# Removing the unread products from TensorE's waits at the ends of two attentions and the starts of two expert stages

## The chip, the cores and the metric

The program runs on one core of one Trainium2 chip. The metric is the device time of one execution in microseconds (us); the kernel before is given by the median of three executions. TensorE runs at one of two clocks here, 1.2 or 2.4 GHz; the profile calls them a granted clock of 0.50 and 1.00.

## The reference

Two transformer layers over x (8 batches, 100 tokens, width 512) with a context of 722 rows per batch. Each layer is a cross attention and a routed feed-forward with a residual around each:

```python
x = x + _L0_xattn_ref(_layernorm(x), ctx_1024, ...)   # 16 heads of 32, causal mask: 100 keys count
x = x + _L0_ffn_ref(_layernorm(x), ...)               # router, best 2 of 8 experts, gelu, width 2048
x = x + _L1_xattn_ref(_layernorm(x), ctx_1024, ...)   # 16 heads of 64, 100 own keys and 722 of the context
x = x + _L1_ffn_ref(_layernorm(x), ...)               # router, best 2 of 8 experts, silu(gate)*up, width 1024
```

## The kernel before, in words

Five stages follow one another, each a block in which every engine has its own written-out program, with a barrier of all engines between blocks: `front` (attention 0 and the routing of its tokens), `experts` for layer 0, `project` (queries, keys and values of layer 1), `attend` (attention 1 and its routing) and `experts` for layer 1; `finish` normalises the last rows.

Precision is kept by splitting float32 operands into a rounded high part and the remainder (`hi`, `lo`) and adding three products. TensorE's program order is the order of the code; where it waits for a semaphore, everything behind stands still.

`front` walks over the batches b = 0 to 7. For one batch TensorE makes the scores (L549, L554), half of the projection of a later pair (`project_half`, L533, only for b up to 5), the values (`values`, 12 products of 512 columns at L511), the router's logits of batch b - 2 (`route_logits`, L617), the output projection of batch b - 1 (`output`, again L511), a rank (`route_rank`, L623 and L624), the transposes of the probabilities (L578), the attended values (L592, L597) and the transposes of the router's rows (`route_turn`, L608). For b = 6 and 7 there is no projection left, and the gap before `values`, which waits for VectorE's `a_y` (the scaled attended rows of the batch before, semaphore `yn`), is filled by `idle_products(6, wo[0])`. Behind the loop come the output of batch 7 and the routing of batches 6 and 7, with three more such calls. An unread product is a matmul into a bank of which nobody reads the result; the bank is written afresh by the next real product with `start=True`:

```python
def idle_products(n, wide):
    for _ in range(n):
        nc.tensor.matmul(ps[:, 7, :], wide[:, 0, 0:128], wide[:, 1, :], start=True, stop=True)
```

What follows the last rank is serial: VectorE turns it into slots, GpSimd scatters the rows to DRAM (`scatter`, L476), SyncE waits for these and loads the first 256 rows of the first expert pass (L434, `e_xs`), and TensorE's `turn(0)` of the next block waits for them.

`experts` runs passes of 256 rows. Ahead of the loop TensorE transposes the first rows (`turn(0)`, 8 transposes at L1157), VectorE and ScalarE copy and split them (L1262 or L1259, L1358, L1268, the last giving `e_xl`), and the first real product (L1188, 256 columns) waits for `e_xl`. In that gap stand 14 unread products of 512 columns (L1171). In a pass each block `kb` is 12 products of 256 columns per up matrix (L1188) and, three blocks later, 6 products of 512 columns (L1165).

`attend` runs over 64 head pairs. After the last one come the last attended values (L2151), the last three products of the output projection (L2168), then the routing of batch 7: `route_turn` (L2187), `route_logits` (L2197), `route_rank` (L2206, L2207). Between these stand 4, 3, 12 and 10 unread products of 362 columns (L2180).

Of the kernel before, what the change touches and what calls it, by code (L numbers as in the profile page):

```python
# [132 lines left out]
def after(eng, sem, n):  # L133

    if type(n) is not int or n > 0:
        eng.wait_ge(sem, n)
# [140 lines left out]
def front(k, ahead0):  # L277

    nc, a, ps = k.nc, k.a, k.ps
# [3 lines left out]
    with ExitStack() as c:  # L283
# [3 lines left out]
        wv, wo = zip(ahead0.hi, ahead0.lo)  # L287
# [66 lines left out]
        def first_half(g, which):  # L354

            return 0 if g == 0 and which == "q" else 2 if g == 0 else 4 * g + (2 if which == "q" else 0)
# [5 lines left out]
        def block_at(b):  # L362

            g = b // 2 + 1
            return (g, "k" if b % 2 == 0 else "q") if g < PAIRS else None

        with nc.Block() as block:
# [138 lines left out]
            def _(pe):  # L506
# [15 lines left out]
                def project_half(g, which, half):  # L522
                    src = xT if which == "q" else ctxT
                    if which == "q":
                        pe.wait_ge(xts, 2 * g + 2)
                    else:
                        pe.wait_ge(ctx_in[g], 32)
                    if g == 0:
                        pe.wait_ge(w_in[which], 16)
                    for mo in (2 * half, 2 * half + 1):  # L530
                        for cc in range(DC):
                            o = 2 * T * (mo % 2)
                            mm = nc.tensor.matmul(ps[:, 6 + half, o:o + 2 * T],  # L533
                                                  w[which][:, cc, 128 * mo:128 * mo + 128], src[g % 2][:, cc, :],
                                                  start=cc == 0, stop=cc == DC - 1)
                    mm.then_inc(pj, 1)

                def scores(b):
                    g, i = b // 2, b % 2
                    pe.wait_ge(pjs, 4 * g + 4)  # L540
                    if b >= 1:
                        pe.wait_ge(ts, 4 * b)
                    if b >= 2:
                        pe.wait_ge(rx, b - 1)
                    if b == 0:
                        pe.wait_ge(rounded, 2)
                    cut = slice(T * i, T * i + T)
                    for q in range(4):
                        nc.tensor.matmul(ps[0:T, q, 0:4 * T], ident_r[:], mask_r[:].rearrange("p f t -> p (f t)"),  # L549
                                         start=True, stop=False)  # L550
                    for f in range(4):
                        for q in range(4):
                            rows_ = slice(HD0 * q, HD0 * q + HD0)
                            mm = nc.tensor.matmul(ps[0:T, q, T * f:T * f + T], qT[g % 2][rows_, f, cut],  # L554
                                                  kT[g % 2][rows_, f, cut], start=False, stop=f == 3)
                    mm.then_inc(s, 1)

                def values(b):
                    g, i = b // 2, b % 2
                    if b == 0:  # L560
                        pe.wait_ge(wld, 1)
                    else:
                        pe.wait_ge(yn, b)
                    pe.wait_ge(cld, g + 1)
                    split_product(4, (ch[g % 2], cl[g % 2]), slice(T * i, T * i + T), wv).then_inc(vd, 1)
# [57 lines left out]
                    nc.tensor.matmul(ps[0:T, 6, 0:E], r.upper[:], r.sel[:], start=True, stop=True)  # L623
                    nc.tensor.matmul(ps[0:T, 6, E:2 * E], ones[0:T, :], r.sel[:], start=True, stop=True).then_inc(rk, 1)  # L624

                def idle_products(n, wide):

                    for _ in range(n):
                        nc.tensor.matmul(ps[:, 7, :], wide[:, 0, 0:128], wide[:, 1, :], start=True, stop=True)

                pe.wait_ge(made_more, 3)
                turn_x(0, 4)
# [9 lines left out]
                for b in range(B):  # L642
                    scores(b)
                    if block_at(b):
                        pe.wait_ge(pjs, first_half(*block_at(b)) - 1)
                        after(pe, rkc, b - 2)
                        project_half(*block_at(b), 0)
                    else:
                        after(pe, rx, b - 1)
                        idle_products(6, wo[0])  # L650
                    values(b)
                    if b == 0:
                        pe.wait_ge(xts, 3)
                        pe.wait_ge(wgs, 1)
                        for cc in range(DC):
                            mm = nc.tensor.matmul(ps[0:T, 5, 0:E], ones[:], wgb[:, cc, :], start=cc == 0, stop=cc == DC - 1)
                        mm.then_inc(lbm, 1)
                        pe.wait_ge(vbw, 1)
                        pe.wait_ge(w_in["o"], 16)
                        pe.wait_ge(lbs, 1)  # L660
                        for cc in range(DC):
                            mm = nc.tensor.matmul(ps[0:T, 5, :], vb_wide[:, cc, :], w["o"][:, cc, :],
                                                  start=cc == 0, stop=cc == DC - 1)
                        mm.then_inc(obm, 1)
                    if b >= 2:
                        if block_at(b):
                            pe.wait_ge(pjs, first_half(*block_at(b)) + 1)
                        route_logits(b - 2)
                    if b >= 1:
                        output(b - 1)  # L670
                    if b >= 2:
                        route_rank(b - 2)
                    if b + 3 < B:
                        pe.wait_ge(pjs, first_half(*block_at(b)))
                        turn_x(b + 3, 7)
                    turn_probabilities(b)
                    if block_at(b):
                        if b + 3 < B:
                            pe.wait_ge(xts, b + 4)
                        else:  # L680
                            pe.wait_ge(pjs, first_half(*block_at(b)))
                        project_half(*block_at(b), 1)
                    if b >= 1 and block_at(b):
                        route_turn(b - 1)
                    attended(b)
                    if not block_at(b):
                        route_turn(b - 1)
                route_logits(B - 2)
                idle_products(10, wo[0])
                output(B - 1)  # L690
                route_rank(B - 2)
                pe.wait_ge(e_hi, 1)
                idle_products(8, ahead0.hi[0])
                route_turn(B - 1)
                route_logits(B - 1)
                pe.wait_ge(rx, B)
                idle_products(5, ahead0.hi[0])
                route_rank(B - 1)

            @block.vector  # L700
# [272 lines left out]
def experts(k, layer, first, then):  # L973
# [6 lines left out]
    nc, a, ps = k.nc, k.a, k.ps  # L980
# [11 lines left out]
    with ExitStack() as c:  # L992
        def parts(name, ready):
            return [[ready[n] if u == 0 and n < len(ready) else
                     k.sb(c, f"{L}{name}{u}_{n}", [128, 4, 512], F32R)[:] for n in range(CH)] for u in range(2)]

        READY = len(first.hi)
        raw, hi, lo = first.raw, parts("hi", first.hi), parts("lo", first.lo)
# [49 lines left out]
        with nc.Block() as block:  # L1048
# [95 lines left out]
            def _(pe):  # L1144
                n = pe.value_load(last, min_val=LEAST, max_val=PASSES)
# [21 lines left out]
                    return mm  # L1167

                turn(0)
                for _ in range(14):  # L1170
                    nc.tensor.matmul(ps[:, 3, :], hi[0][0][:, 0, 0:128], hi[0][0][:, 1, :], start=True, stop=True)  # L1171
                with pe.Fori(0, n) as j:
                    for kb in range(NB):
                        if True:
# [6 lines left out]
                            for i in range(len(ups)):  # L1181
# [5 lines left out]
                                for t, (w, x, cc) in enumerate(terms):  # L1187
                                    mm = nc.tensor.matmul(ps[:, bank, 0:CAP], w[:, cc, cut], x[:, cc, :],  # L1188
                                                          start=t == 0, stop=t == len(terms) - 1)
# [27 lines left out]
                if not gated:  # L1217
                    pe.wait_ge(m_split, 4 * DC)
                    for p in range(2):
                        for half, (start, wide) in enumerate(HALVES):  # L1220
                            for cc in range(DC):
                                for t, (w, x) in enumerate(((then.wm_first_hi, then.even[0]), (then.wm_first_hi, then.even[1]),
# [3 lines left out]
                                                          start=cc == 0 and t == 0, stop=cc == DC - 1 and t == 2)  # L1226
# [669 lines left out]
def attend(k, s1, ahead1):  # L1896

    nc, a, ps = k.nc, k.a, k.ps
    WIDE = [(0, 512), (512, KEYS - 512)]
    QK_SLOTS, V_SLOTS, P_SLOTS = 2, 3, 3  # L1900
    MEMORY = 2 * T
# [4 lines left out]
    with ExitStack() as c:  # L1906
# [3 lines left out]
        qk_hi = [k.sb(c, f"a1_qk_hi{u}", [128, T + KEYS], F32R) for u in range(QK_SLOTS)]  # L1910
# [62 lines left out]
        with nc.Block() as block:  # L1973
# [102 lines left out]
            def _(pe):  # L2076
# [97 lines left out]
                    keys_copied(b + 1, OUTPUT_AT)  # L2174
                    output_part(b, range(IC)).then_inc(od, 1)

                def idle_products(n):

                    for _ in range(n):
                        nc.tensor.matmul(ps[:, 0, 0:362], qk_hi[0][:, 0:128], qk_hi[0][:, MEMORY:MEMORY + 362],  # L2180
                                         start=True, stop=True)

                def route_turn(b):
                    pe.wait_ge(rn, b + 1)
# [65 lines left out]
                turn(PAIRS - 1, IC - 1, 0)  # L2250
                output_part(B - 1, range(IC - 2, IC - 1))
                turn(PAIRS - 1, IC - 1, 1)
                idle_products(4)
                attended(PAIRS - 1, B - 1, IC - 1)
                idle_products(3)
                output_part(B - 1, range(IC - 1, IC)).then_inc(od, 1)
                idle_products(12)
                route_turn(B - 1)
                route_logits(B - 1)
                idle_products(10)  # L2260
                route_rank(B - 1)

            @block.vector
# [331 lines left out]
```

## Time and profile before

| what | value |
|---|---|
| median of three runs | 1688.87 us (1685.06 to 1690.17) |
| the profiled execution, its time | 1687.72 us |
| its span, first to last instruction | 1685.8 us |
| mean granted TensorE clock | 0.968 |
| TensorE busy | 1571.0 us, 93% of the span |
| VectorE busy | 1147.8 us, 68% |
| ScalarE, GpSimd busy | 823.2 us (49%), 279.0 us (17%) |
| unread products | 35 (front), 14 and 14 (the two expert stages), 29 (attention 1): 92 of 12292 matmul records |

The time is the span and about 1.9 us around it. A busy share of 93% says which engine carries most of the program, not that each of its instructions is useful: the unread products are counted as busy. The granted clock beside the busy share tells at which speed that work was done.

### The profile page before, as it was taken

To read this page: it belongs to the slowest core of one execution; us is meant where nothing else is said; L and a number is where in the kernel's file an instruction comes from. 1 tells how busy PE (TensorE), PEld (TensorE's weight loads), DVE (VectorE), ACT (ScalarE), POOL (GpSimd) and SP (SyncE) were. 2 spreads that over 40 slices of the span, in tenths; PEclk is the share of its full clock that TensorE was granted. 3 is DMA by queue.
4 is the path that set the end of the run, shared out by engine and by line. 5 is a ranking of instruction groups with operands and counts; after the bars stand their busy time and mean duration, and the time that the engine had idled before them with its cause. 6 is when DMAs were issued, how large, how long until landed. Compare 5 with 4: busy or idle time off the path is not lost.

```text
span 1685.8 us, 33006 instructions
## 1 busy us (share of the span) xinstructions
PE 1571.0 (93%) x12292; PEld 1404.1 (83%) x12292; DVE 1147.8 (68%) x2134; ACT 823.2 (49%) x1544; POOL 279.0 (17%) x317
## 2 busy tenths in 40 slices
PE   7998699999999879989999999999999869999991
PEld 6886589999999779779898888888888669999991
DVE  4886687777777552267676676768676567677774
ACT  3453355555555432266555555656564434445442
POOL 2104241101000030211111111111111041121112
PEclk9999799999999979999999999999999979999996
DMA  7997466666666444231120112020203046657753
GB/s 254 363 392 228 141 227 230 213 214 207 215 217 209 139 152 153 101 104 37 33 56 25 52 29 61 17 64 16 61 22 98 16 168 216 210 187 225 230 179 90
DMA packets 94076, 246.60 MB, mean 146 GB/s; under 512 B 32614, under 2 KB 39782, under 8 KB 78870
## 3 DMA queue, kind: packets, MB, share of 16 engines
q1 hardware_dynamic: 84758, 223.67, 39.0%
q0 software_dynamic: 9216, 21.53, 5.7%
q8 instruction: 69, 1.13, 0.3%
q14 instruction: 33, 0.27, 0.0%
HBM read 179.66 MB, written 65.50 MB: 145 GB/s over the span
## 4 chain that ended last, share of the span: by engine, by line
PE 46%; DVE 6%; ACT 2%; DMA 1%; issue 1%; POOL 0%; DVEq 0%; POOLq 0%; ACTq 0%; SPq 0%
PE banks L2090 12%; PE banks L1188 10%; PE banks L1165 5%; PE banks L2151 4%; PE banks L2135 4%; PE banks L2124 4%; PE banks L2111 3%; PE banks L2168 3%; ACT a_P L2437 1%; DVE a_nmax L2289 1%; DMA token_sums<-e_y,e_dest 1%; DVE a_qk_lo L2283 1%; PE banks L1157 1%; DVE a_P L2298 1%; DVE a_PT L2305 0%
## 5 line engine op out<-in xcount | busy, mean ns | idle before, releaser
L2090 PE MATMUL banks<-a_ch,a_wm 128*128 128x362 f32 x992 | 276.0, 339 | 0.0
L1252 DVE TENSOR_TENSOR e_lo<-e_raw,e_hi 128x2048 fp32r<-128x2048 f32 x97 | 224.6, 2316 | 48.9 <-ACT e_hi L1341 46.3
L1188 PE MATMUL banks<-e_xh,e_hi 128*128 128x256 f32 x768 | 216.9, 282 | 1.5 <-DVE e_lo L1252 1.0
L1188 PE MATMUL banks<-e_xl,e_hi 128*128 128x256 f32 x768 | 216.1, 281 | 0.0
L1188 PE MATMUL banks<-e_xh,e_lo 128*128 128x256 f32 x768 | 215.8, 281 | 0.0
L1341 ACT CAST e_hi<-e_raw 128x2048 fp32r<-128x2048 f32 x98 | 185.8, 1904 | 15.3 <-PE banks L1165 13.4
L2090 PEld LDWEIGHTS banks<-a_ch,a_wm 128*128 128x128 f32 x992 | 179.6, 189 | 0.4 <-issue 0.4
L1136 POOL DMA_INDIRECT token_sums<-e_y,e_dest x32 | 74.9, 2340 | 551.9 <-DVE e_y L1309 288.4
L2090 PE MATMUL banks<-a_cl,a_wm 128*128 128x362 f32 x496 | 163.1, 329 | 0.0
L1188 PEld LDWEIGHTS banks<-e_xh,e_hi 128*128 128x128 f32 x768 | 145.2, 189 | 10.4 <-DVE e_lo L1252 4.8
L1165 PE MATMUL banks<-e_hi,e_hh 128*128 128x512 f32 x384 | 152.7, 398 | 1.0 <-DVE e_hl L1286 1.0
L1165 PE MATMUL banks<-e_lo,e_hh 128*128 128x512 f32 x384 | 151.1, 393 | 0.0
L1165 PE MATMUL banks<-e_hi,e_hl 128*128 128x512 f32 x384 | 150.7, 392 | 0.0
L1188 PEld LDWEIGHTS banks<-e_xl,e_hi 128*128 128x128 f32 x768 | 145.4, 189 | 5.5
L1188 PEld LDWEIGHTS banks<-e_xh,e_lo 128*128 128x128 f32 x768 | 145.4, 189 | 0.0
L2437 ACT ACTIVATE a_P<-banks,a_nmax 100x822 f32<-100x822 f32 x128 | 120.6, 952 | 28.9 <-DVE a_nmax L2289 28.9
L1385 ACT ACTIVATE e_hf<-banks,e_b 128x256 f32<-128x256 f32 x128 | 60.6, 474 | 144.5 <-PE banks L1188 144.4
L2289 DVE TENSOR_REDUCE a_nmax<-banks 100x1 f32<-100x822 f32 x128 | 123.4, 1005 | 4.3 <-PE banks L2124 4.1
L2283 DVE TENSOR_TENSOR a_qk_lo<-a_mem,a_qk_hi 128x722 fp32r<-128x722 f32 x64 | 59.0, 924 | 90.5 <-ACT a_qk_hi L2431 86.2
L2135 PE MATMUL banks<-ident,a_P 100*128 100x100 f32 (+2 forms) x896 | 100.7, 252 | 2.1 <-ACT a_PT L2445 2.0
L2135 PEld LDWEIGHTS banks<-ident,a_P 100*128 100x128 f32 (+2 forms) x896 | 81.1, 136 | 18.3 <-issue 15.9
L2090 PEld LDWEIGHTS banks<-a_cl,a_wm 128*128 128x128 f32 x496 | 94.3, 190 | 0.0
(314 smaller groups left out, 3435.7 us busy)
## 6 DMA issues: line engine op xcount, KB each, us to landing
e_raw<-wout SPq DMA_DIRECT2D x50, 1024.0 KB, 6.8
e_raw<-w SPq DMA_DIRECT2D x34, 1024.0 KB, 6.7
slot_rows<-a_zero SPq DMA_DIRECT2D x66, 514.0 KB, 9.9
e_raw<-wgate SPq DMA_DIRECT2D x17, 1024.0 KB, 5.0
e_raw<-wup SPq DMA_DIRECT2D x17, 1024.0 KB
a_craw<-ctxT SPq DMA_DIRECT2D x28, 361.0 KB
e_xs<-slot_rows SPq DMA_DIRECT2D x9, 514.0 KB, 6.5
a_craw<-slot_rows SPq DMA_DIRECT2D x9, 514.0 KB
```

Source lines behind the costliest of these rows:

```text
L1136: pool.indirect_dma_start(out=k.sums[layer][:, :], out_offset=bass.IndirectOffsetOnAxis(ap=dest[:, s:s + 1], axis=0), in_=y[:, s, :], in_o ...
L1165: mm = nc.tensor.matmul(ps[:, 4 + s, :], h[q % 4][:, cut], w[:, q % 4, :], start=q == 0 and t == 0, stop=q == NB - 1 and t == 2)
L1188: mm = nc.tensor.matmul(ps[:, bank, 0:CAP], w[:, cc, cut], x[:, cc, :], start=t == 0, stop=t == len(terms) - 1)
L1252: nc.vector.tensor_tensor(lo[g % 2][i], raw[q % RAW], hi[g % 2][i].bitcast(F32), ALU.subtract)\
L1341: nc.scalar.copy(hi[g % 2][i], raw[q % RAW]).then_inc(hi_done, 1)
L2090: mm = nc.tensor.matmul(ps[:, 6 + half, 0:wide], w[:, cc, cut], x[:, cc, start:start + wide], start=cc == 0 and t == 0, stop=cc == DC - 1 ...
L2124: mm = nc.tensor.matmul(ps[0:T, 2 * two + f, 0:wide], x[r, 0:T], y[r, T + first:T + first + wide], start=t == 0, stop=t == 2)
L2135: mm = nc.tensor.transpose(ps[0:size, 4 + n // 5, T * (n % 5):T * (n % 5) + T], P[(2 * p + two) % P_SLOTS][:, first:first + size], k.ident ...
L2151: mm = nc.tensor.matmul(ps[HD1 * two:HD1 * two + HD1, 6, 384:384 + T], v[s][0:size, n, HD1 * two:HD1 * two + HD1], PT[two][0:size, n, :], ...
L2283: nc.vector.tensor_tensor(qk_lo[s][:, MEMORY:], mem[s][:], qk_hi[s][:, MEMORY:].bitcast(F32), ALU.subtract).then_inc(k_l, 1)
L2289: nc.vector.tensor_reduce(nmax[:, h:h + 1], two_banks(2 * two)[0:T, 0:KEYS], AX, ALU.max, negate=True)\
L2437: nc.scalar.activation(P[(2 * p + two) % P_SLOTS][:], two_banks(2 * two)[0:T, 0:KEYS], ACT.Exp, bias=nmax[:, h:h + 1], accum_out=sums[:, h ...
```

## The change

All eight calls of `idle_products` (29 unread products in the tail of `attend`, 35 at batches 6 and 7 and in the tail of `front`), the two helpers and the loop of 14 ahead of each expert stage's passes go. Nothing else is edited; every wait stays where it was, `pe.wait_ge(e_hi, 1)` and `pe.wait_ge(rx, B)` in the tail of `front` too.

```diff
@@ front, TensorE
-                def idle_products(n, wide):
-                    for _ in range(n):
-                        nc.tensor.matmul(ps[:, 7, :], wide[:, 0, 0:128], wide[:, 1, :], start=True, stop=True)
...
                     else:
                         after(pe, rx, b - 1)
-                        idle_products(6, wo[0])
                     values(b)
...
                 route_logits(B - 2)
-                idle_products(10, wo[0])
                 output(B - 1)
                 route_rank(B - 2)
                 pe.wait_ge(e_hi, 1)
-                idle_products(8, ahead0.hi[0])
                 route_turn(B - 1)
                 route_logits(B - 1)
                 pe.wait_ge(rx, B)
-                idle_products(5, ahead0.hi[0])
                 route_rank(B - 1)
@@ experts, TensorE
                 turn(0)
-                for _ in range(14):
-                    nc.tensor.matmul(ps[:, 3, :], hi[0][0][:, 0, 0:128], hi[0][0][:, 1, :], start=True, stop=True)
                 with pe.Fori(0, n) as j:
@@ attend, TensorE
-                def idle_products(n):
-                    for _ in range(n):
-                        nc.tensor.matmul(ps[:, 0, 0:362], qk_hi[0][:, 0:128], qk_hi[0][:, MEMORY:MEMORY + 362],
-                                         start=True, stop=True)
...
                 turn(PAIRS - 1, IC - 1, 1)
-                idle_products(4)
                 attended(PAIRS - 1, B - 1, IC - 1)
-                idle_products(3)
                 output_part(B - 1, range(IC - 1, IC)).then_inc(od, 1)
-                idle_products(12)
                 route_turn(B - 1)
                 route_logits(B - 1)
-                idle_products(10)
                 route_rank(B - 1)
```

On TensorE, at the very end of `front`, the order of the instructions stands like this, the removed ones with a minus (L623 and L624 are the rank of batch 6 and then of batch 7, L608 and L617 the transposes and logits of batch 7):

```order
 L623 MATMUL banks<-r_sel,r_upper 100x8
 L624 MATMUL banks<-r_sel,a_ones 100x8
-L629 MATMUL banks<-e_hi_0 128x512 x8
 L608 MATMUL banks<-ident,r_rows 128x100 x4
 L617 MATMUL banks<-r_wg_gamma,r_xT 100x8 x4
-L629 MATMUL banks<-e_hi_0 128x512 x5
 L623 MATMUL banks<-r_sel,r_upper 100x8
 L624 MATMUL banks<-r_sel,a_ones 100x8
```

The real instructions keep their order; only the filling between them is gone.

## Rows read from the trace of the kernel before

**Rows 1.** The page, part 2: TensorE's granted clock in 40 slices, in tenths.

```profile
PEclk9999799999999979999999999999999979999996
```

**Rows 2.** Timeline of attention 1's tail (start us, us, engine, line, count).

```profile
1342.29 1.43 PE L2151 MATMUL banks<-a_PT,a_v 100*64 100x100 f32 x28 [0.41 <-issue]
...
1345.13 2.14 PE L2180 MATMUL banks<-a_qk_hi 128*128 128x362 f32 x12
...
1349.53 0.93 PE L2187 MATMUL banks<-ident,r_rows 100*128 100x100 f32 x4 [2.25 <-DVE r_rows L2338]
1350.49 0.49 ACT L2467 COPY a_craw<-banks 128x400 f32<-128x400 f32 x1 [0.37 <-PE banks L2187]
1351.04 1.50 PE L2197 MATMUL banks<-r_wg,a_craw 128*100 128x8 f32 x8 [0.58 <-ACT a_craw L2467]
1352.39 3.37 PE L2180 MATMUL banks<-a_qk_hi 128*128 128x362 f32 x10
1352.58 0.17 DVE L2343 COPY logits<-banks 100x8 f32<-100x8 f32 x1 [0.91 <-PE banks L2197]
...
1356.31 0.16 DVE L240 TENSOR_TENSOR r_rank<-r_taken,banks 100x8 f32<-100x8 f32 x1 [0.35 <-PE banks L2207]
```

**Rows 3.** Stretches of 1 us: PE, PEld, DVE, ACT, POOL busy, then PEclk, DMA share, GB/s.

```profile
175.00:176.00 1.00, 1.00 (x5) 0.71 (x5) 0.96 (x3) 0.00 (x0) 0.00 (x0) 0.83 0.00 0
...
202.00:203.00 1.00, 1.00 (x5) 0.78 (x4) 0.36 (x1) 1.00 (x2) 0.00 (x0) 0.68 1.03 393
...
1370.00:1371.00 1.00, 1.00 (x6) 0.82 (x5) 0.80 (x1) 1.00 (x2) 1.00 (x2) 1.00 1.02 418
```

**Rows 4.** Timeline of front, batch 6 and, last row, 7: unread and values' products.

```profile
135.71 2.58 PE L629 MATMUL banks<-e_hi 128*128 128x512 f32 x6
137.28 0.57 DVE L753 TENSOR_TENSOR a_y<-banks,a_rec 128x400 f32<-128x400 f32 x1
...
138.14 0.39 PE L511 MATMUL banks<-e_hi,a_ctxhi 128*100 128x512 f32 x1
...
140.64 0.39 PE L511 MATMUL banks<-e_hi,a_ctxlo 128*100 128x512 f32 x1
...
151.89 1.66 PE L629 MATMUL banks<-e_hi 128*128 128x512 f32 x6
```

**Rows 5.** Timeline of front's tail: logits of batch 6, output and routing of batch 7.

```profile
169.81 1.50 PE L617 MATMUL banks<-r_wg_gamma,r_xT 128*100 128x8 f32 x8 [3.87 <-ACT r_xT L918]
...
173.07 0.58 DVE L756 TENSOR_TENSOR a_y_lo<-a_y,a_y_hi 128x400 fp32r<-128x400 f32 x1 [0.59 <-ACT a_y_hi L914]
...
175.47 0.39 PE L511 MATMUL banks<-e_hi,a_y_hi 128*100 128x512 f32 x1
...
181.88 0.56 PE L608 MATMUL banks<-ident,r_rows 100*128 100x100 f32 x4 [1.20 <-DVE r_rows L776]
...
182.48 0.49 ACT L918 COPY r_xT<-banks 128x400 f32<-128x400 f32 x1
...
183.02 0.87 PE L617 MATMUL banks<-r_wg_gamma,r_xT 128*100 128x8 f32 x8 [0.58 <-ACT r_xT L918]
...
183.93 0.17 DVE L787 TENSOR_TENSOR logits<-banks,r_lbias 100x8 f32<-100x8 f32 x1 [0.56 <-PE banks L617]
```

**Rows 6.** Timeline of the heads of both expert stages.

```profile
197.95 1.94 PE L1157 MATMUL banks<-ident,e_xs 128*128 128x128 f32 x8 [10.71 <-DMA e_xs<-slot_rows]
...
202.64 1.23 DVE L1268 TENSOR_TENSOR e_xl<-e_xf,e_xh 128x1024 fp32r<-128x1024 f32 x1 [1.21 <-ACT e_xh L1358]
...
204.28 0.28 PE L1188 MATMUL banks<-e_xh,e_hi 128*128 128x256 f32 x1
...
1366.39 1.97 PE L1157 MATMUL banks<-ident,a_craw 128*128 128x128 f32 x8 [10.12 <-DMA a_craw<-slot_rows]
...
1370.20 1.23 DVE L1268 TENSOR_TENSOR e_xl<-e_xf,e_xh 128x1024 fp32r<-128x1024 f32 x1 [1.04 <-ACT e_xh L1358]
...
1372.24 0.28 PE L1188 MATMUL banks<-e_xh,a_wm 128*128 128x256 f32 x1
```

**Rows 7.** The page, part 5: largest group of the expert passes (busy, mean ns, idle before).

```profile
L1188 PE MATMUL banks<-e_xh,e_hi 128*128 128x256 f32 x768 | 216.9, 282 | 1.5 <-DVE e_lo L1252 1.0
```

## The prediction

> **What bounds the kernel now.** I read the page first. In its row of the clock 36 of 40 slices stand at 9 [rows 1]. The fifth has 7 and holds 169 to 211 us, the tail of `front` and the head of the first expert stage; the 33rd has 7 and holds 1349 to 1391 us, the tail of attention 1 and the head of the second. These are the places of the edit; the other two dips, in the 15th and the last slice, are not touched. Then come the timelines there, which show what each unread product stands between, and stretches of 1 us, which show when the clock moved. The reader is to look for two things: what releases the real instruction behind the unread products, and at which clock it then runs. In the expert stages the largest group sat idle for 1.5 us ahead of 768 products [rows 7], so what is lost at the head of such a stage is paid at the end of the program. The tails are serial: TensorE's `turn(0)` waited 10.71 and 10.12 us for the rows that the tail's last rank lets GpSimd scatter and SyncE load [rows 6], so a late rank makes everything late by the same amount.
>
> **What the low clock costs.** Twelve unread products of 362 columns took 2.14 us at a clock of 1.00, ten took 3.37 us at 0.50 [rows 2]. Take off the last product's own length (0.32 and 0.65 us) and the spacing is 1.82/11 = 0.165 us against 2.72/9 = 0.302 us, a factor of 1.83. A stretch of S us at the low clock therefore does the work of S/1.83 and loses 0.45 S. The values' 12 products of 512 columns had a spacing of (140.64 - 138.14)/11 = 0.227 us [rows 4]; at the low clock I estimate 0.227 x 1.83 = 0.416 us, 0.19 us more each; the six unread ones just before, with (2.58 - 0.39)/5 = 0.44 us, lie near that. The Trainium skill, page "TensorE: Matmul & The Clock Gate", section Terms, prices throttled time at (1 - K/N), which is 0.50 S here; with it the slow stretches below would cost a tenth more, some 0.6 us over the whole sum. I go by the rows.
>
> **How long the low clock lasts.** Three rises can be timed from the first product of the work that led to them: 169.81 us [rows 5] to about 175.2 (the stretch 175 to 176 has 0.83), 5.4 us; 197.95 us [rows 6] to about 202.6 (202 to 203 has 0.68), 4.7 us; 1366.39 us to 1370.0 at the latest (1370 to 1371 has 1.00), 3.6 us [rows 3, 6]. In all three the unread products were what ran on while the real work waited. Without them I count such a stretch anew from the first real product of the dense work: 3.6 to 5.4 us, and I take 4.5 us for the heads.
>
> **Part by part.**
>
> (1) Batch 6 of `front`, 6 unread products. They ran from 135.71 us; `a_y`, for which the real products wait, was there at 137.28 + 0.57 = 137.85, and the first of them started at 138.14, by then at the full clock [rows 4]. Without filling it starts 0.2 us earlier, but TensorE has stood for about 2 us before it, and the clock was low there, as the spacing of 0.44 us says. With a rise 3.6 us later 3.6/0.416 = 8.7 products are slow: 8.7 x 0.19 = 1.65, less 0.2 = **+1.4 us**. Bounds: -0.2 (the clock is up anyway) and 12 x 0.19 - 0.2 = +2.1. These products precede the output projection of batch 5, the rank and the transposes on TensorE, and VectorE's addition waits for that projection, so I see no cover.
>
> (2) Batch 7, the same call. The clock was already up: six products in 1.66 us, spaced (1.66 - 0.39)/5 = 0.25 us [rows 4]. The gap without them is about as short. I take 0; the price of the other case is a rival below.
>
> (3) Ahead of the output of batch 7, 10 unread products. `y_lo` was ready at 173.07 + 0.58 = 173.65, but the output began at 175.47 [rows 5]: here the filling delayed real work by 1.8 us. Now it starts at once, at the low clock: 8 to 12 slow products cost 1.5 to 2.3 us. Net -0.3 to +0.5; I take **+0.2 us**.
>
> (4) Ahead of the transposes and logits of batch 7, 8 unread products; ahead of the last rank, 5. With them the clock was up for both: transposes' start to ScalarE's copy 182.48 - 181.88 = 0.60 us, logits' start to VectorE's read 183.93 - 183.02 = 0.91 us [rows 5]. The same two steps at the low clock in attention 1: 1350.49 - 1349.53 = 0.96 and 1352.58 - 1351.04 = 1.54 us [rows 2]. That tail had idled for 2.25 us before them and was slow; here the pause becomes over 3 us. So **+1.0 us** (0 if the clock holds). The last rank was no longer covered by the 5, and I take nothing for it.
>
> (5) Head of the first expert stage, 14 unread products. `e_xl` was ready at 202.64 + 1.23 = 203.87 and the first real product started at 204.28, at 1.00 [rows 3, 6]. Without filling: 0.35 us earlier, then 4.5 us low, 0.45 x 4.5 = 2.0; **+1.7 us**. Bounds: S of 1 to 5.4 us gives +0.1 to +2.1. VectorE and ScalarE take up the results of the first blocks, so their work starts later too; no queue of SyncE's is moved, the weight loads hang on the same semaphores.
>
> (6) Tail of attention 1, 4 + 3 + 12 + 10. The first two sit in gaps of under 1 us. The 12 ended 2 us before the transposes and did not keep the clock, which was at 0.50 for transposes and logits; nothing to lose there. The 10 ran slowly into the last rank, for which VectorE waited 0.35 us [rows 2]: **-0.3 us**. Upper bound: the clock falls earlier and the 28 attended products (1.43 us) and the 3 of the output run slowly, 1.2 + 0.6 = +1.8.
>
> (7) Head of the second expert stage. Ready at 1370.20 + 1.23 = 1371.43, started at 1372.24 [rows 6]: the filling cost 0.75 us. Net 2.0 - 0.75 = **+1.3 us**; with S of 1 to 5.4, -0.3 to +1.7.
>
> Sum: 1.4 + 0 + 0.2 + 1.0 + 1.7 - 0.3 + 1.3 = **+5.3 us**. Against the profiled execution's 1687.72 us that is 1693.0. That execution lies 1.15 us under the median of the runs, 1688.87, so a median of 1694.2, which I round to **1694.0 us**, 0.3% more. About 0.3% (5.1 us) is what a measurement of this kernel can tell from no change, so the forecast sits just above that line.
>
> **The rivals.**
>
> - *The clock falls in more places.* Batch 7 runs its 12 values slowly too (12 x 0.19 = +2.3), or the end of attention 1 does (+1.8 in place of -0.3), and the slow stretches are 5.4 us instead of 4.5 (+0.4 each). For it: the low clock came after a pause of some 3 us in the tails, and every us of delay shifts the later gaps. Against: the gaps at batch 7 are under 2 us and dense products stand around them. About +8.5 us, 1697.4.
> - *The heads warm nearly as fast as before.* `turn(0)` has just run, and the low stretch after the first real product is only 2 us: heads +0.55 and +0.15; and (4) loses half. Sum about 1.4 + 0.2 + 0.5 + 0.55 - 0.3 + 0.15 = +2.5 us, down to +1 without (1): 1690 to 1691.4. The first 1.94 us of the five before the rise at 202.6 were such transposes [rows 6], which does not tell the two apart.
> - *The filling was only in the way* (the other side). Real work stood behind unread products for 0.2 + 1.8 + 0.35 + 0.3 + 0.75 = 3.4 us in all. If the clock rises with real work as soon as it did before, all of it is gained: 1688.9 - 3.4 = 1685.5, a gain within what can be told. It wins from the point where the low stretches lose less than these 3.4 us together, that is, less than 7.6 us of low clock over all places. Against: I expect some 4 us at each of three places.
>
> **How the numbers follow.** My forecast 0.50, the first rival 0.20, the second 0.22, the third 0.08. The forecast's own case spreads over 2.5 us to either side and its centre is just over the line: two thirds of it (0.33) slower, the rest no change. Of the first rival 0.18 is slower, of the second 0.03, of the third 0.03 faster. So slower 0.54, within 0.3% 0.43, faster 0.03. The range: from the second rival's low end, 1690, less a microsecond for the spread of the runs, 1689.0, to the first rival with all heads at their upper bound, 1700.0.
>
> **What would show it.** Granted clock of 0.50 in the stretches from 204 to 208 us and after 1371 us, with products of 256 columns spaced 0.21 us instead of 0.12; the first real product at `e_xl`'s end; VectorE's first read of the logits of batch 7 in `front` 1.5 us after their start; the last rank of attention 1 without a wait. The distance from the last scatter to `turn(0)` should be unchanged, and so should the expert passes and the 64 steps of attention 1 once they run. I am wrong if the clock is at 1.00 within 2 us of the first real product of an expert stage, or if the two tails come out no longer than before.

## The result and the profile after

| | before | after |
|---|---|---|
| median | 1689.09 us (1685.06 to 1691.21, 5 runs) | 1697.07 us (1696.12 to 1699.7, 5 runs) |
| profiled execution | 1687.72 us | 1696.12 us |
| span | 1685.8 us | 1694.3 us |
| mean granted clock | 0.968 | 0.959 |

The ratio of the times is 1.0053, 95% interval 1.0038 to 1.0067, so the change costs 8.9 us (6.4 to 11.3). The forecast of 1694.0 us and its sum of +5.3 us had the right sign and were too small.

The page of the kernel after, TensorE's busy time, the granted clock, and the group that answers to [rows 7]:

```profile
PE 1554.1 (92%) x12200; PEld 1390.3 (82%) x12200; DVE 1147.7 (68%) x2134; ACT 823.2 (49%) x1544; POOL 281.1 (17%) x317
...
PEclk9998599999999979999999999999999969999996
```

```profile
L1178 PE MATMUL banks<-e_xh,e_hi 128*128 128x256 f32 x768 | 218.2, 284 | 6.6 <-DVE e_xl L1258 4.2 <-DVE e_lo L1242 2.4
```

TensorE is busy for 17 us less and the program is 8.5 us longer: what went was unread work, and the clock went with it. Against [rows 1] the fourth slice, which holds batch 6, fell from 9 to 8, the fifth from 7 to 5 and the 33rd from 7 to 6.

TensorE's timeline in `front` (L511 is the values of batch 6 and then the output of batch 7, L608 and L617 the transposes and logits of batch 7):

```profile
138.63 0.72 PE L511 MATMUL banks<-e_hi,a_ctxhi 128*100 128x512 f32 x1 [2.18 <-issue]
139.14 0.63 PE L511 MATMUL banks<-e_lo,a_ctxhi 128*100 128x512 f32 x1
139.57 0.63 PE L511 MATMUL banks<-e_hi,a_ctxlo 128*100 128x512 f32 x1
...
177.20 0.75 PE L511 MATMUL banks<-e_hi,a_y_hi 128*100 128x512 f32 x1 [2.38 <-DVE a_y_lo L748]
...
186.07 0.90 PE L608 MATMUL banks<-ident,r_rows 100*128 100x100 f32 x4 [3.24 <-issue]
187.55 1.50 PE L617 MATMUL banks<-r_wg_gamma,r_xT 128*100 128x8 f32 x8 [0.58 <-ACT r_xT L910]
```

The values of batch 6 now start behind 2.18 us of idle time and are spaced 0.43 us, where [rows 4] had 0.227; they stay so to the twelfth. The output of batch 7 starts 2.4 us behind the last work instead of behind ten unread products, and the transposes and logits run at the low clock: from their start to ScalarE's copy (187.01 us) and VectorE's read (189.09 us) it is 0.94 and 1.54 us, where [rows 5] gave 0.60 and 0.91.

The heads of the two expert stages, TensorE:

```profile
203.54 1.94 PE L1149 MATMUL banks<-ident,e_xs 128*128 128x128 f32 x8 [11.09 <-DVEq L1221]
209.69 0.58 PE L1178 MATMUL banks<-e_xh,e_hi 128*128 128x256 f32 x1 [4.21 <-DVE e_xl L1258]
210.06 0.42 PE L1178 MATMUL banks<-e_xl,e_hi 128*128 128x256 f32 x1
210.28 0.41 PE L1178 MATMUL banks<-e_xh,e_lo 128*128 128x256 f32 x1
...
1373.86 1.97 PE L1149 MATMUL banks<-ident,a_craw 128*128 128x128 f32 x8 [10.18 <-DMA a_craw<-slot_rows]
1380.07 0.58 PE L1178 MATMUL banks<-e_xh,a_wm 128*128 128x256 f32 x1 [4.24 <-DVE e_xl L1258]
```

Stretches of 1 us after these starts (PE, PEld, DVE, ACT, POOL busy, PEclk, DMA share, GB/s):

```profile
209.00:210.00 1.00, 0.32 (x1) 0.32 (x2) 0.45 (x1) 1.00 (x1) 0.00 (x0) 0.50 1.05 404
213.00:214.00 1.00, 1.00 (x11) 1.00 (x10) 0.57 (x1) 0.32 (x1) 0.92 (x2) 0.99 0.97 410
...
235.00:236.00 1.00, 1.00 (x6) 1.00 (x6) 1.00 (x1) 0.00 (x0) 0.00 (x0) 0.50 0.70 246
...
1383.00:1384.00 1.00, 1.00 (x7) 1.00 (x7) 0.12 (x1) 0.00 (x0) 1.00 (x1) 0.60 0.00 0
```

The real products begin within 0.3 us of `e_xl` and at the low clock, spaced 0.21 us, and the clock is up again at 213.0 and 1383.8 us, that is 3.3 and 3.7 us after the first of them. The row at 235 us was not foreseen: inside the first expert pass the clock falls once more, for 3.4 us (233.5 to 236.9). It follows waits of TensorE that the view of waits over 205 to 245 us shows (us in total, times, the longest):

```profile
PE banks L1178 <- DVE e_xl L1258: 4.2, 1, 4.2
PE banks L1178 <- DVE e_lo L1242: 2.4, 2, 2.0
PE banks L1157 <- DVE e_hl L1276: 0.9, 1, 0.9
```

The tail of attention 1, answering to [rows 2]:

```profile
1357.33 0.93 PE L2172 MATMUL banks<-ident,r_rows 100*128 100x100 f32 x4 [4.25 <-DVE r_rows L2319]
1358.84 1.50 PE L2182 MATMUL banks<-r_wg,a_craw 128*100 128x8 f32 x8 [0.58 <-ACT a_craw L2448]
...
1363.71 0.16 DVE L240 TENSOR_TENSOR r_rank<-r_taken,banks 100x8 f32<-100x8 f32 x1
```

As slow as in [rows 2], and the last rank waits for nothing: from the logits' start to the rank it is 4.87 us, before it was 5.27.

### The profile page after: what moved, and what is told of

Same layout as the page of the kernel before. It is cut to its first block, busy times and chain, and to the rows that moved or that the text cites. A ratio compares the mean times of both kernels' runs of the same rounds, so it can differ in the third digit from the quotient of the medians.

```text
span 1694.3 us, 32823 instructions
## 1 busy us (share of the span) xinstructions
PE 1554.1 (92%) x12200; PEld 1390.3 (82%) x12200; DVE 1147.7 (68%) x2134; ACT 823.2 (49%) x1544; POOL 281.1 (17%) x317
## 4 chain that ended last, share of the span: by engine, by line
PE 45%; DVE 6%; ACT 2%; DMA 1%; issue 1%; POOL 0%; DVEq 0%; POOLq 0%; ACTq 0%; SPq 0%
PE banks L2080 12%; PE banks L1178 11%; PE banks L1157 5%; PE banks L2141 4%; PE banks L2125 4%; PE banks L2114 4%; PE banks L2101 3%; PE banks L2158 3%; ACT a_P L2418 1%; DVE a_nmax L2270 1%; DVE a_qk_lo L2264 1%; DMA token_sums<-e_y,e_dest 1%; DVE a_P L2279 1%; PE banks L1149 1%; DVE a_PT L2286 0%
## 5 line engine op out<-in xcount | busy, mean ns | idle before, releaser
L1128 POOL DMA_INDIRECT token_sums<-e_y,e_dest x32 | 80.5, 2517 | 556.7 <-DVE e_y L1299 295.1
L1178 PEld LDWEIGHTS banks<-e_xh,e_hi 128*128 128x128 f32 x768 | 146.5, 191 | 15.4 <-DVE e_lo L1242 5.4
L2418 ACT ACTIVATE a_P<-banks,a_nmax 100x822 f32<-100x822 f32 x128 | 120.6, 952 | 28.5 <-DVE a_nmax L2270 28.5
L1178 PE MATMUL banks<-e_xh,a_wm 128*128 128x256 f32 x512 | 92.9, 283 | 5.9 <-DVE e_xl L1258 4.2
```

The costliest lines, as they stand in the source:

```text
L1128: pool.indirect_dma_start(out=k.sums[layer][:, :], out_offset=bass.IndirectOffsetOnAxis(ap=dest[:, s:s + 1], axis=0), in_=y[:, s, :], in_o ...
L2418: nc.scalar.activation(P[(2 * p + two) % P_SLOTS][:], two_banks(2 * two)[0:T, 0:KEYS], ACT.Exp, bias=nmax[:, h:h + 1], accum_out=sums[:, h ...
```

## The experiments

The experiments ran in three sets, each on a chip of its own, where the kernel before takes 1679.1, 1687.3 and 1678.8 us; each ratio is against the kernel before on the same chip. To price the parts I also measured, in every trace, the time between two starts of VectorE instructions that all traces have. A stretch counts as filled where its unread products are as before, and as unfilled where they are gone or have 8 columns, whatever was done elsewhere. Left out are, at the first head, the traces with GpSimd's split moved or with more filling there, and at the tail of attention 1 and the second head those with more filling there (one of these, the first kernel of "More filling", is kept at the second head, where its filling is as before):

| stretch (times of the trace before) | filled, mean (n) | unfilled, mean (n) | cost | predicted |
|---|---|---|---|---|
| batches 6 and 7, 137.28 to 160.15 | 22.98 (10) | 25.39 (4) | +2.4 | +1.4 |
| tail of `front`, 173.07 to 187.71 | 14.87 (10) | 15.94 (4) | +1.1 | +1.2 |
| first head, 202.64 (`e_xl`) to 240.57 | 38.69 (7) | 41.85 (3) | +3.2 | +1.7 |
| tail of attention 1, 1341.24 to 1368.40 | 26.19 (8) | 26.72 (3) | +0.5 | -0.3 |
| second head, 1370.20 (`e_xl`) to 1400.46 | 30.13 (8) | 31.37 (4) | +1.2 | +1.3 |

The costs add up to 8.4 us, against 8.9 (6.4 to 11.3) by the times. At both heads and at batches 6 and 7 every unfilled trace is longer than every filled one. At the tail of `front` the two overlap (14.3 to 15.9 us filled, 15.4 to 16.4 unfilled), and at the tail of attention 1 too, so these two costs are the least certain. A single pair of traces would mislead: the stretch between the heads (240.57 to 1341.24), which the change does not touch, takes 1098.1 to 1101.8 us in the traces that leave the split in place, and it was 2.0 us shorter in the trace after than in the one before.

**The parts alone.** Only the filling of `front` (35 products), of both heads (28), or of attention 1 (29) is removed, each exactly as in the change. For `front`:

```diff
-                        idle_products(6, wo[0])
...
-                idle_products(10, wo[0])
...
-                idle_products(8, ahead0.hi[0])
...
-                idle_products(5, ahead0.hi[0])
```

> The unread products go from `front` alone (6 + 6 + 10 + 8 + 5). Clock theory: the 12 values' products of batch 6 and the 12 output products of batch 7 run at 0.50, and so do the transposes and logits of batch 7; turn(0) of the first expert stage comes 4 to 6 us later than before, and the time grows by 4 to 6 us. Theory that the loss comes from the instruction stream having been shifted (another place of its loads or of a stall), not from the clock: less than 2 us, or a shift that is not at these products.

> The 14 unread products go from the heads of both expert stages alone. Clock theory: each head's first 12 products of 256 columns are spaced 0.21 us, 1.3 to 2.5 us are lost at the first head and about 1 us at the second, +2.5 to +3.5 us in all; some of it may come back in the first pass, where VectorE is the slower engine. If VectorE's chain covers it: under +1 us.

> The 29 unread products go from attention 1's tail alone. Clock theory: the clock was at 0.50 there for transposes, logits and rank with them as well, so nothing is lost and the 0.35 us wait for the last rank goes: -0.3 us, no change that the timing can tell. Theory that these products kept the clock for the last attended values and the last output products: +1.8 us, with these at 0.50.

Measured against 1679.11 us (29 runs): `front` 1682.61 us, ratio 1.0023 (1.0012 to 1.0033), +3.9 us; the heads 1682.74 us, 1.0019 (1.0010 to 1.0028), +3.2 us; attention 1680.32 us, 1.0011 (1.0002 to 1.0021), +1.9 us. The three add up to 0.53% (0.36 to 0.70), the size of the whole change, so no interplay between the parts shows that is larger than this interval. Attention was expected to gain 0.3 us, or to lose 1.8 by the other theory, and it lost.

**The same instructions, little work.** All 92 stay, each with 8 columns. One of the three places:

```diff
-nc.tensor.matmul(ps[:, 7, :], wide[:, 0, 0:128], wide[:, 1, :], start=True, stop=True)
+nc.tensor.matmul(ps[:, 7, 0:8], wide[:, 0, 0:128], wide[:, 1, 0:8], start=True, stop=True)
```

> All 92 unread products stay, but each has 8 columns in place of 512 or 362: the same instructions in the same places, with almost no time on the array. Clock theory: the array is as idle as without them, so the time is that of the changed kernel, +6 to +9 us, with the same products at 0.50. Theory of the shifted instruction stream: the stream is that of the kernel before, so the time is the one of before, within 1.5 us.

Measured: 1685.62 us, ratio 1.0045 (1.0032 to 1.0058), +7.6 us. Most of the loss, by the medians of the ratios 0.45% of 0.53%, comes with all 92 instructions in place, so it does not come from a shifted instruction stream; what the unread products do is keep TensorE's array at work. The page of this kernel shows the fifth slice at 5 and the 33rd at 6, as after the change:

```profile
PEclk9999599999999989999999999999999969999996
```

**`front` in two halves.** Either the two calls of 6 go, or the 10, the 8 and the 5.

> Only the two calls of 6 at batches 6 and 7 of `front` go. Clock theory: a few of the 24 values' products run at 0.50, +1 to +3 us. If the gaps are too short for the clock to fall: 0 to +0.3 us.

> Only the calls of 10, 8 and 5 in the tail of `front` go. Clock theory: output of batch 7 slow but begun earlier (0 to +0.8 us), transposes and logits of batch 7 slow (+1.0 us): +1 to +2 us. With the set before, the two parts should add to its +3.9 us (ratio 1.0023). If these products were only in the way: -1.8 us.

Measured against 1687.33 us (29 runs): 1688.97 us, 1.0007 (0.9992 to 1.0021), and 1689.22 us, 1.0008 (0.9995 to 1.0021). The runs alone settle neither: both intervals reach from a small gain to 3.5 us. They do exclude the 1.8 us that the second would have gained if its products had only been in the way. The stretches above do better. Batches 6 and 7 took 25.76 us in the first (22.75 to 23.09 in nine filled traces, 24.23 in one), the tail of `front` 16.41 us in the second (14.34 to 15.93 filled). Split at 144.55, the two batches share the loss. Batch 6 takes 7.2, 8.7, 8.7 and 10.0 us in the four traces without its filling, 7.4 on average with it: +1.3 us. Batch 7 takes 17.1 us in three of them and 15.6 in the trace of the kernel after, and 15.6 in every trace with filling: +1.1 us. In those three the clock fell within a microsecond of the first value of batch 7, which is the first rival's mechanism. In the trace of the kernel after it did not fall there, and all of batch 6's values ran low instead; in the trace without any of `front`'s filling batch 6's values kept the high clock.

**The tail of attention 1 has two outcomes.** Two kernels that are the same there, with the same idle time, from the same chip; first the kernel before, run again, then the one without `front`'s 10, 8 and 5:

```profile
1352.69 0.93 PE L2187 MATMUL banks<-ident,r_rows 100*128 100x100 f32 x4 [2.24 <-DVE r_rows L2338]
1354.20 1.50 PE L2197 MATMUL banks<-r_wg,a_craw 128*100 128x8 f32 x8 [0.58 <-ACT a_craw L2467]
```

```profile
1351.93 0.56 PE L2184 MATMUL banks<-ident,r_rows 100*128 100x100 f32 x4 [2.24 <-DVE r_rows L2335]
1353.08 0.87 PE L2194 MATMUL banks<-r_wg,a_craw 128*100 128x8 f32 x8 [0.58 <-ACT a_craw L2464]
```

Behind the same pause the clock is low in one execution and high in the other. With the filling the stretch took 27.0 to 27.2 us in three traces and 25.6 to 25.7 in five; without it always 26.7 to 26.8. So the filling loses 0.3 us (the late rank) or gains 1.1, and gains on average. The trace on which I predicted showed the bad outcome. Without the filling the pause ahead of the transposes is 4.2 us (3.0 with the 8 columns), and the clock was low behind it in all three traces.

**Why the first head costs more than the second.** GpSimd's split of `Wm` and the context, which runs beside the first expert pass, is moved behind the loop over the passes, in a kernel with the filling and in one without the 14 products.

```diff
-                if not gated:
-                    pool.wait_ge(m_in, 32)
...
                     pool.wait_ge(y_out, j * 32 + 32)
                     pool.sem_inc(y_free, 1)
+                if not gated:
+                    pool.wait_ge(m_in, 32)
...
                 pool.sem_inc(stored, 1)
```

> All unread products stay. GpSimd's split of Wm's first part and of the context into two halves each, which runs from about 206 to 232 us beside the first expert's pass, is moved behind the loop over the passes; this costs some 15 to 25 us at the stage's end and is the control for the next kernel. The kernels without the 14 products took 40.9 to 42.5 us from VectorE's e_xl of the first pass to the first e_hh of the second group of blocks (202.64 to 240.57 in the profile of before), those with them 37.9 to 39.6. Both theories: with VectorE undisturbed this stretch falls to about 36 to 38 us here.

> As the kernel before it, but without the 14 products behind the transposes of both expert stages. Theory A, the low clock alone makes the loss at the first head: the stretch is longer than the control's by the same 3 us or so as with the split at its old place, and TensorE's wait for e_lo near 215 us stays about 2 us. Theory B, the loss is doubled because the late first products meet VectorE slowed by GpSimd's split: the stretch is longer than the control's by 1.3 to 2.0 us only, as at the second head (1.4 us measured there), TensorE waits under 0.5 us for e_lo, and the clock does not fall a second time in the first pass.

Measured, one execution each: 1694.55 and 1700.17 us against 1678.82; the 16 us are the split at the stage's end, as expected. The stretch takes 35.09 us with the filling, less than the 36 to 38 expected, and 37.34 without, a difference of 2.3 instead of 3.2. TensorE waits for no `e_lo` in either, and the clock does not fall a second time in the first pass. VectorE's group `e_lo` over the first pass (busy us, mean ns of one), in the kernel before and in the one with the split moved, shows what the split does to it:

```profile
L1252 DVE TENSOR_TENSOR e_lo<-e_raw,e_hi 128x2048 fp32r<-128x2048 f32 x7 | 17.0, 2430 | 1.3 <-ACT e_hi L1341 1.2
```

```profile
L1252 DVE TENSOR_TENSOR e_lo<-e_raw,e_hi 128x2048 fp32r<-128x2048 f32 x6 | 13.7, 2290 | 6.1 <-ACT e_hi L1341 6.1
```

One `e_lo` takes VectorE 2.3 us by itself and 2.4 to 3.8 us beside GpSimd's split. So theory B holds in its mechanism: beside the split VectorE is late with `e_lo` and TensorE waits for it. The longest such wait is 0.5 to 1.8 us in the seven filled traces, and the clock stays up. It is 2.0 us in two of the three unfilled ones, and the clock falls a second time for 3.4 us; it is 1.4 us in the third, the kernel with 8 columns, and the clock stays up. The second kernel of "More filling" has its filling and a wait of 2.1 us, and there the clock falls a second time too. So the second fall goes with the long wait and not with the missing products themselves. The third unfilled trace also gives the cost of a head without the second fall, 40.94 - 38.69 = 2.3 us, the same as with the split moved. The size is less certain: 2.3 is over the 1.3 to 2.0 expected, and the excess of 3.2 - 2.3 = 0.9 us that is put down to the wait and the second fall rests on few traces. The split beside the pass costs 3.6 us there with the filling (38.69 against 35.09) and 4.5 without (41.85 against 37.34). To place it in a later pass was not tried.

**More filling.** Three kernels try to close the gaps that the filling of before leaves. The first adds 26 unread products behind `front`'s last rank and 36 behind attention's, and makes the 12 ahead of attention's transposes 20. The second has 40 for the 36, 8 for the 10, and fills on both sides of the first transposes of an expert stage; the third adds to the second 14, 20, 8, 3 and 8 around the barrier into the project stage. From the second kernel:

```diff
                 route_rank(B - 1)
+                idle_products(40)
...
+                idle_up(5)
                 turn(0)
-                for _ in range(14):
-                    nc.tensor.matmul(ps[:, 3, :], hi[0][0][:, 0, 0:128], hi[0][0][:, 1, :], start=True, stop=True)
+                idle_up(15)
```

> All unread products stay and more are added where TensorE waits: 26 of 512 columns behind the last rank of `front` and 36 of 362 columns behind that of attention 1, both while it waits for the barrier, and 20 in place of 12 ahead of the transposes of batch 7 in attention 1. Clock theory: turn(0) of both expert stages runs at 1.00 (1.0 us in place of 1.95), transposes and logits of attention 1's tail too (-1.0 us), the last rank no longer waits: -2 to -3.5 us. If TensorE enters the barrier late: up to +2 us.

> More unread products than before: 26 behind the front's last rank, 40 behind the attention's, 5 ahead of the first transposes of both expert stages and 15 behind them instead of 14, 20 instead of 12 ahead of the attention's last transposes, 8 instead of 10 ahead of its last rank. If the clock's state is what these products are for, the transposes and the first 16 products of both stages run at the high clock: 0.6 and 1.9 us less at each head, 3 to 5 us less than before in all (ratio 0.997 to 0.998). If the products only stand in the way, it is slower by what they hold up, about 1 us (1.0005). The barriers between the stages can take some of it back: with 26 and 36 they came at most 0.5 us later.

> As the kernel before it, and also unread products around the barrier into the project stage, where the clock is low from 585 to 609 us: 14 behind the memory's products, 20 ahead of the first transposes, 8, 0 and 3 between the next ones, 8 ahead of the first product of the projection. If they hold the clock, the first 10 products there take 0.17 instead of 0.33 us and the transposes of two rows half as much: 1.5 to 3 us less than the kernel before it (ratio to before 0.996 to 0.997). If the barrier or the transposes come later for them, no gain or a loss of up to 1 us.

| kernel | median, kernel before | ratio (95%) | granted clock |
|---|---|---|---|
| first | 1688.10, 1687.33 us | 0.9993 (0.9979 to 1.0006) | 0.972 |
| second | 1681.39, 1678.82 us | 1.0017 (1.0008 to 1.0026) | 0.975 |
| third | 1679.84, 1678.82 us | 1.0007 (0.9996 to 1.0018) | 0.981 |

None is a gain that can be told, where 2 to 3.5, 3 to 5 and 5 to 7 us were expected if the clock is held, and the second is a loss of 2.9 us whose interval leaves out no change. One part did what it was for: with 20 products instead of 12 ahead of attention's transposes the pause is 0.9 us instead of 2.24, and the clock was high for transposes and logits in all three traces. The rest gave and took. In the second kernel the second head takes 28.4 us instead of 30.1, and the first gains nothing (38.9 against 38.7). But from `front`'s last rank to `e_xl` it is 17.1 us instead of some 15.0, and the tail of attention 1 takes 28.5 us instead of 26.2. Together that is +2.9 us, as measured. TensorE of this kernel, and then SyncE's queue:

```profile
1348.08 8.85 PE L2185 MATMUL banks<-a_qk_hi 128*128 128x362 f32 x40
1359.20 2.44 PE L1172 MATMUL banks<-a_wm 128*128 128x512 f32 x5 [2.27 <-issue]
1361.43 1.63 PE L1158 MATMUL banks<-ident,a_craw 128*128 128x128 f32 x8
```

```profile
1354.33 0.38 SPq L2027 DMA_DIRECT2D a_craw<-slot_rows  x1
1358.33 0.31 SPq L1085 DMA_DIRECT2D e_lb<-bet  x1
```

The clock had fallen before the 40, which therefore took 8.85 us instead of 6.6. They ended at 1356.93 us, 2.6 us after SyncE had issued the rows' load, and the barrier of all engines waited for them: from that load to SyncE's next one, in the next block, it is 4.0 us, where the kernel before has 2.8. Then the 5 stood ahead of `turn(0)`, at the low clock. From the last rank to `turn(0)` it is 13.2 us (1348.27 to 1361.43), before 10.1. At the first stage the products ended early enough (SyncE's loads lie 3.1 us apart, as before), but TensorE had no instruction across the barrier for 4.96 us, the clock fell in it, and the 5 held up `turn(0)`: 12.45 us from the last rank (180.42) instead of 10.2.

```profile
181.62 4.01 PE L629 MATMUL banks<-e_hi 128*128 128x512 f32 x17
190.60 2.47 PE L1172 MATMUL banks<-e_hi 128*128 128x512 f32 x5 [4.96 <-issue]
192.87 1.91 PE L1158 MATMUL banks<-ident,e_xs 128*128 128x128 f32 x8
```

In the third kernel the clock held across the barrier into `project` and for its transposes, and fell at 597.54 us, behind a pause of 1.93 us and just as the work it was meant for had begun, whose first products are spaced 0.33 us as they were without:

```profile
592.99 0.56 PE L1701 MATMUL banks<-ident,p_xn 100*128 100x100 f32 x4 [0.28 <-DVE p_xn L1802]
593.34 2.11 PE L1710 MATMUL banks<-a_ch 128*128 128x512 f32 x8
597.38 0.52 PE L1732 MATMUL banks<-p_xh,p_hi 128*128 128x400 f32 x1 [1.93 <-issue]
597.69 0.54 PE L1732 MATMUL banks<-p_xl,p_hi 128*128 128x400 f32 x1
```

The stretch from `project`'s first statistics to attention's `a_mem` (590.39 to 731.11 before) is 139.1 us in the second kernel and in the third, so the third kernel's filling gained nothing there. Among the other traces it varies from 138.6 to 140.7 us.

## Why the prediction was right in sign and too small

- **Price of the low clock**: held. The values of batch 6 are spaced 0.43 us at the low clock (estimated 0.416), the products of 256 columns 0.21 instead of 0.12.
- **Length of the low stretch**: held. From the first real product of a head to the clock's rise it is 3.3 to 6.0 us in the eight heads without filling, 4.7 on average, where I took 4.5; in the 16 heads with filling (eight traces) the clock was up 1.2 to 3.1 us before that product.
- **(1) and (2), batches 6 and 7**: +2.4 for +1.4. On average batch 6 cost +1.3, as forecast, but that is a mean of very different outcomes (-0.2, +1.3, +1.3 and +2.6); in the profiled kernel all twelve of its values ran low, from 138.63 to 143.4 us. The missing term is batch 7, at +1.1 on average, which I had put at nothing ("the gap without them is about as short"). The gap is short, but in three traces of four the clock fell at its end. This step, a term put at nothing, failed.
- **(3) and (4), the tail of `front`**: +1.1 for +1.2. The 1.8 us by which the 10 products held up the output of batch 7 belong to the traces with the pause near 165 us (last section). In the filled traces without it the output starts 0.06 us behind `y_lo`, so the products delay nothing there.
- **(5), the first head**: +3.2 for +1.7, above my bound of 2.1. This is the largest miss. The step that failed is "0.45 x 4.5": it prices the products that run slowly and stops there. In the pass that follows TensorE meets a VectorE that works beside GpSimd's split, and in two traces of three a wait of 2.0 us and a second low stretch of 3.4 us came of it (by my own factor, 1.5 us). Where neither came, the formula comes near: the kernel with 8 columns had a low stretch of 6.0 us, which gives 0.45 x 6.0 - 0.35 = 2.4 us for the 2.3 measured, and with the split moved the stretch was 5.0 us, which gives 1.9 for 2.3. In the profiled pair the stretch grew by 4.2 us (37.93 to 42.14), since the trace before was among the shorter filled ones (37.8 to 39.6).
- **(6), the tail of attention 1**: +0.5 by the traces, +1.9 (0.3 to 3.5) by the times, for -0.3. "Nothing to lose there" was read off one execution, and another behind the same pause keeps the clock. Which of the two sizes is nearer stays open. In the profiled pair the -0.3 came true, because both traces show the low clock there.
- **(7), the second head**: +1.2 for +1.3.
- **The rivals**: the first ("the clock falls in more places") is right in part, and its 1697.4 us is next to the 1697.07 measured, which is partly luck. Batch 7 did run slowly, for +1.1 on average instead of +2.3; it put the rest on the end of attention 1 (+1.8, measured +0.5) and on stretches of 5.4 us (measured 4.7), and had no term for the first pass. "Warm nearly as fast" falls: it took 2 us of low clock at a head, and the shortest of eight was 3.3. "Only in the way" falls with it: these stretches alone are more than its 7.6 us of low clock, and the program got slower.

## What to carry to other kernels

Unread work in a wait is worth what the real work behind it loses at the low clock, less what it holds up; both are read from the spacing of the real products and from the start of the first one against its operand. Where an engine is the bound and starts late at a low clock, price the waits that the delay makes in the steady part behind it as well. More filling is not more gain: count what each call stands ahead of, a barrier of all engines included, and judge by the time, not by the mean granted clock.

## What the runs showed of the hardware that was not expected

- Behind the same pause of 2.24 us the clock was low in one execution and high in another; so one trace gives one of two outcomes for such a place. The 29 runs of the kernel before on one chip had granted clocks of 0.962 to 0.970, and a line through them falls by 1.0 us for each 0.001; on the two other chips, with 0.968 to 0.972, it falls by 0.8 and 0.3.
- The last kernel, with a mean clock of 0.981, was no faster than the kernel before with 0.968 to 0.972 on the same chip. The mean counts all stretches alike, and the filling that raised it also held up `turn(0)`.
- In the traces before and after and in all of the second set VectorE stands idle for some 4 us near 165 us, ScalarE for over 6, and VectorE again near 131 us; in the first and third set they don't, and the kernel is 8 to 10 us faster there. VectorE's reciprocal behind it, in the kernel before and in the one without the heads' filling on another chip:

```profile
169.21 2.66 DVE L751 RECIPROCAL a_rec<-banks 128x400 f32<-128x400 f32 x1 [4.05 <-remote]
```

```profile
161.96 2.65 DVE L751 RECIPROCAL a_rec<-banks 128x400 f32<-128x400 f32 x1
```

  The profile calls the releaser remote; what it is stays open. The kernel before, profiled once more on the second chip (1689.41 us), shows both pauses again. Where the second one comes, the clock was low ahead of the output of batch 7 in the kernel before too (168.5 to 175.3 us).
- Across the barriers into the two expert stages TensorE had no instruction for 4.96 and 2.27 us in the second kernel (2.27 where it came last to the barrier), and filling on both sides did not hold the clock. Across the barrier into `project` it was 1.32 us in the third kernel, and the clock held.
